# Two vector instructions in place of two GpSimd ones, and small VectorE instructions in other chunks of a fused Mamba, attention and expert kernel

## The reference, cut to what matters

```python
def mamba(x):                                    # x is already layer-normed once
    residual = x
    xz = layernorm(x, in_alpha, in_bias) @ in_proj_w.T + in_proj_b
    x_in, z = split(xz)
    x_conv = silu(causal_conv4(x_in) + conv_b)   # 512 channels
    B, C = split(x_conv @ x_proj_w.T + x_proj_b) # 16 states
    dt = clip(softplus(x_conv @ dt_proj_w.T + dt_proj_b), 1e-4, 10)
    for t in range(1024):
        h = exp(clip(dt * A, -10, 0)) * h + dt * B * x_conv
        if t % 16 == 15: h = h * min(1, 10 / norm(h))      # norm over the 16 states
        y = sum(C * h) + D * x_conv
    out = (y * silu(z)) @ out_proj_w.T + out_proj_b
    return norm_alpha * (residual + out - mean) / (std + 1e-6) + norm_bias   # the closing norm

def experts(x):                                  # 16 experts, the top 6 of a softmax
    p, i = top_k(softmax(x @ router_w.T + router_b), 6)
    gate = scatter(p / (sum(p) + 1e-10), i)
    acc = max(sum(gate), 1e-10)
    return sum(x @ expert_w[e] * gate[e] for e in range(16)) / acc + 1e-10 * sum(p)
```

## Time and profile before

| | |
|---|---|
| median of three runs | 4976.51 us |
| the profiled execution, its time | 4979.03 us |
| its span, first to last instruction | 4977.2 us |
| granted TensorE clock over the span | 0.952 |
| busy: PE, DVE, ACT, POOL | 4396.3, 3774.0, 2928.0, 2691.3 us |
| in 100 to 3150 us (most of the first stage): PE, DVE, ACT, POOL | 2761.8, 2683.7, 2397.4, 2574.0 of 3050 us |
| period of a pair of tiles in the steady loop | about 100 us |

### The profile page before, as it was taken

How to read it: one execution, slowest core, us unless ns; L and a number is a source line. 1 busy time by engine, 2 the same in 40 slices (tenths; PEclk the granted TensorE clock), 3 DMA queues, 4 the chain that set the end, 5 groups by cost and what they waited for, 6 DMA issues and landing times.

```text
span 4977.2 us, 83341 instructions
## 1 busy us (share of the span) xinstructions
PE 4396.3 (88%) x22592; PEld 3061.0 (62%) x22592; DVE 3774.0 (76%) x9556; ACT 2928.0 (59%) x8578; POOL 2691.3 (54%) x1412
## 2 busy tenths in 40 slices
PE   5899998899989998999899989877776779999999
PEld 4777777777777776777677777634434444444444
DVE  3898988888888888888889889953333357777776
ACT  5877787777777777778777778724444421111111
POOL 3888888888888888888888888810000000000000
PEclk8999999999999999999999999988888989999999
DMA  2111111111111111111111111100100100000000
GB/s 95 53 54 49 52 50 52 48 50 51 52 51 47 55 48 55 45 53 49 53 49 53 50 53 49 50 31 26 51 25 30 42 25 19 17 19 18 17 19 16
DMA packets 119406, 214.06 MB, mean 43 GB/s; under 512 B 19232, under 2 KB 85664, under 8 KB 118560
## 3 DMA queue, kind: packets, MB, share of 16 engines
q1 hardware_dynamic: 119072, 211.10, 12.9%
HBM read 184.83 MB, written 26.21 MB: 42 GB/s over the span
## 4 chain that ended last, share of the span: by engine, by line
PE 39%; issue 19%; DVE 17%; POOL 16%; ACT 6%; DMA 1%; DVEq 1%; SPq 1%; POOLq 0%; ACTq 0%
PE ps L644 21%; POOL prod L342 8%; POOL hb L350 5%; DVE macc L957 3%; ACT zr L408 3%; PE ps L771 3%; PE ps L695 2%; PE ps L621 2%; PE ps L674 2%; PE ps L750 2%; DVE sc L1108 1%; DVE dtt L1113 1%; PE ps_dA L771 1%; PE ps L681 1%; POOL u L359 1%
## 5 line engine op out<-in xcount | busy, mean ns | idle before, releaser
L644 PE MATMUL ps<-w_x,mxT 128*128 128x512 f32 x4096 | 1893.1, 601 | 21.8 <-DVE macc L957 21.8
L864 DVE TENSOR_TENSOR_SCAN hb<-ps_dA,hb 128x1088 f32<-128x1088 f32 x512 | 1240.6, 2423 | 164.7 <-issue 103.3
L342 POOL TENSOR_TENSOR prod<-hb,cbc 128x1024 f32<-128x1024 f32 x512 | 1120.2, 2188 | 408.4 <-DVE hb L883 408.4
L408 ACT ACTIVATE zr<-dt,aneg 128x128 f32<-128x128 f32 x4096 | 1240.8, 388 | 69.8 <-DVE dt L1007 69.8
L350 POOL TENSOR_TENSOR hb<-u,bbc 128x1024 f32<-128x1024 f32 x512 | 1199.7, 2343 | 84.2 <-POOL prod L342 72.1
L644 PEld LDWEIGHTS ps<-w_x,mxT 128*128 128x128 f32 x4096 | 745.7, 193 | 725.3 <-issue 654.2
L957 DVE SCALAR_TENSOR_TENSOR macc<-ps,gate,macc 128x256 f32<-128x256 f32 x2048 | 977.5, 477 | 246.9 <-PE ps L644 180.5
L621 PEld LDWEIGHTS ps<-prod,ident 128*128 128x128 f32 x8192 | 979.1, 198 | 254.0 <-POOL prod L342 194.2
L621 PE MATMUL ps<-prod,ident 128*128 128x128 f32 x8192 | 997.1, 282 | 142.5 <-POOL prod L342 142.5
L417 ACT ACTIVATE ps_dA<-zr 128x1024 f32<-128x1024 f32 x512 | 518.3, 1012 | 0.0
L424 ACT ACTIVATE sq<-hb 128x64 f32<-128x64 f32 x512 | 159.6, 312 | 450.8 <-DVE hb L864 447.2
(11 more groups left out here) (184 smaller groups left out, 5014.3 us busy)
## 6 DMA issues: line engine op xcount, KB each, us to landing
bbc<-bcd SPq DMA_DIRECT2D x128, 512.0 KB, 3.8
cbc<-bcd SPq DMA_DIRECT2D x128, 512.0 KB, 3.5
xt<-in_x SPq DMA_DIRECT2D x128, 128.0 KB, 3.0
x2d<-macc SPq DMA_DIRECT2D x64, 128.0 KB, 1.7
xcv<-x2d SPq DMA_DIRECT2D x64, 128.0 KB, 2.1
x3d<-x1b SPq DMA_DIRECT2D x64, 128.0 KB, 1.9
x1b<-x3d SPq DMA_DIRECT2D x64, 128.0 KB, 2.0
out_dram<-macc SPq DMA_DIRECT2D x64, 128.0 KB, 1.7
```

The source lines that it names most:

```text
L342: TT(dst, states, cc, ALU.mult).then_inc(M["prodp"], 1)
L408: last = act(zr[k][:, s, :], dt[:, s // N, :], ACT.Relu, bias=10.0, scale=aneg[:, s:s + 1])
L644: last = mm(banks[p % len(banks)][:], mxT[k][:, j, :], w_x[:, j, p * 512:(p + 1) * 512], start=(j == 0), stop=(j == KD - 1))
L864: V.tensor_tensor_scan(states, dA, states, 0.0, ALU.mult, ALU.add).then_inc(M["scan"], 1)
```

## The change

Five edits. The 20 small tensor_scalar instructions that build the diagonals become two tensor_tensor ones over broadcast operands. o1 moves from chunk 1 to the end of chunk 0. The closing norm is computed as `((oo - mean) * alpha) * (1 / (std + eps)) + beta` by two scalar_tensor_tensor instructions on the DVE, in chunks 3 and 4; the POOL's two are gone, and its residual sum moves from chunk 6 to chunk 7. den is a tensor_scalar with a per-partition scalar instead of a scalar_tensor_tensor; selp moves to just before the gate in chunk 7; route_norm1 moves behind dt's bias, and ACT's side of it behind dt's exp and log. ACT computes the deviation ahead of the squares of chunk 3.

```diff
@@ POOL, extra
-                if c == 4 and "B" in stages:
-                    g.wait_ge(M["o3"], AHEAD + i)
-                    TT(oo[:], oo[:], ga_row[:], ALU.mult).then_inc(M["o4"], 1)
+                if c == 7 and "B" in stages:
                     g.wait_ge(M["o4"], AHEAD + i)
-                    TT(oo[:], oo[:], be_row[:], ALU.add).then_inc(M["o5"], 1)
-                if c == 6 and "B" in stages:
-                    g.wait_ge(M["o5"], AHEAD + i)
                     g.wait_ge(R["ac"], AHEAD + (i - 3) * (X + 1) + 1)
                     TT(x1b[1 - k][:], oo[:], xt[1][:], ALU.add).then_inc(M["x1"], 1)
@@ ACT, step
                 for c in range(NC):
+                    if c == 3 and B:
+                        a.wait_ge(M["vc3"], AHEAD + i)
+                        act(sc[:, 9:10], sc[:, 8:9], ACT.Ln).then_inc(M["ln3"], 1)
+                        a.wait_ge(M["ln3"], AHEAD + i)
+                        act(sc[:, 10:11], sc[:, 9:10], ACT.Exp, scale=0.5).then_inc(M["sd3"], 1)
                     if S_:
                         squares(i, c)
...
-                        if B:
-                            a.wait_ge(M["vc3"], AHEAD + i)
-                            act(sc[:, 9:10], sc[:, 8:9], ACT.Ln).then_inc(M["ln3"], 1)
-                            a.wait_ge(M["ln3"], AHEAD + i)
-                            act(sc[:, 10:11], sc[:, 9:10], ACT.Exp, scale=0.5).then_inc(M["sd3"], 1)
...
                     if c == 7:
-                        if B:
-                            route_norm(i - 1)
                         if F:
                             a.wait_ge(M["dtb"], AHEAD + (i + 3) * EB)
                             act(dtt[:], dtt[:], ACT.Exp).then_inc(M["edt"], 1)
                             a.wait_ge(M["edt"], AHEAD + i + 3)
                             act(dtt[:], dtt[:], ACT.Ln, bias=1.0).then_inc(M["ldt"], 1)
+                        if B:
+                            route_norm(i - 1)
@@ DVE, route_gate (the step with selp is gone from route_step)
+                v.wait_ge(R["router"], AHEAD + n * ROUTER + 6)
+                TT(selp[:], ex[:, 0:X], rest[:, 0:X], ALU.subtract).then_inc(R["router"], 1)
                 v.wait_ge(R["router"], AHEAD + n * ROUTER + 14)
                 TS(gate[k][:], selp[:], ms[:, 11:12], None, ALU.mult).then_inc(R["router"], 1)
@@ DVE, step: chunks 0, 3, 4, 7
                     TS(dt[:], dtt[:], 1e-4, 10.0, ALU.max, ALU.min).then_inc(M["dt"], 1)
+                if B:
+                    v.wait_ge(M["xr"], AHEAD + i * 16)
+                    v.wait_ge(M["x1"], AHEAD + i - 1)
+                    STT(oo[:], xt[1][:], r1b[1 - k][:], ob_row[:], ALU.mult, ALU.add).then_inc(M["o1"], 1)
                 end(0)
...
-                    TS(oo[:], oo[:], mv[:, 2, 0:1], sc[:, 12:13], ALU.subtract, ALU.mult).then_inc(M["o3"], 1)
+                    STT(oo[:], oo[:], mv[:, 2, 0:1], ga_row[:], ALU.subtract, ALU.mult).then_inc(M["o3"], 1)
                 end(3)
...
+                if B:
+                    v.wait_ge(M["o3"], AHEAD + i)
+                    STT(oo[:], oo[:], sc[:, 12:13], be_row[:], ALU.mult, ALU.add).then_inc(M["o4"], 1)
                 end(4)
...
-                    STT(sc[:, 6:7], sc[:, 4:5], 1e-6, sc[:, 5:6], ALU.mult, ALU.add).then_inc(M["den"], 1)
+                    TS(sc[:, 6:7], sc[:, 4:5], 1e-6, sc[:, 5:6], ALU.mult, ALU.add).then_inc(M["den"], 1)
@@ DVE, ahead of the loop
-            for e in range(EB):
-                for t in range(TAPS):
-                    TS(dcw[:, e * TAPS + t, :], ident[:], cw[:, e, t:t + 1], None, ALU.mult).then_inc(s_zero, 1)
-                TS(ddp[:, e, :], ident[:], dpar[:, e:e + 1], None, ALU.mult).then_inc(s_zero, 1)
+            for dst, w in ((dcw, cw[:].rearrange("p e t -> p (e t)")), (ddp, dpar[:])):
+                n = dst.shape[1]
+                TT(dst[:], ident[:].rearrange("p (a c) -> p a c", a=1).broadcast_to([P, n, P]),
+                   w.rearrange("p (a c) -> p a c", c=1).broadcast_to([P, n, P]), ALU.mult).then_inc(s_zero, 1)
```

More of the change, by code:

```diff
@@ L149, in build @@
         dve_m = ("st1", "mv1", "vp", "den", "sx1", "xn", "keep", "xib", "zb", "xcc", "bcv", "dtb", "dt", "scan", "nr",
-                 "st0", "hs", "yg", "o1", "o2", "st3", "mv3", "vc3", "se3", "r3", "o3")
+                 "st0", "hs", "yg", "o1", "o2", "st3", "mv3", "vc3", "se3", "r3", "o3", "o4")
         act_m = ("carry", "lnp", "r1", "qs", "xnTs", "ez", "lz", "ss", "ex", "lx", "sx", "edt", "ldt", "zr", "dA", "sq", "nl",
                  "ne", "ln3", "sd3")
-        pool_m = ("sz", "xcv", "u", "bt", "prodp", "o4", "o5", "x1")
+        pool_m = ("sz", "xcv", "u", "bt", "prodp", "x1")
         pe_m = ("xnT", "xi", "z", "conv", "bc", "dtp", "y", "op")
@@ L447, in route_init @@
             def route_init(n, k, stored):
-                a.wait_ge(R["router"], AHEAD + n * ROUTER + 12)
+                a.wait_ge(R["router"], AHEAD + n * ROUTER + 11)
                 stored()
@@ L923, in route_step @@
                 elif step == 5:
-                    v.wait_ge(R["router"], AHEAD + n * ROUTER + 6)
-                    TT(selp[:], ex[:, 0:X], rest[:, 0:X], ALU.subtract).then_inc(R["router"], 1)
-                elif step == 6:
                     v.wait_ge(R["router"], AHEAD + n * ROUTER + 5)
                     TS(ms[:, 6:7], ms[:, 5:6], ms[:, 4:5], 1e-10, ALU.mult, ALU.add).then_inc(R["router"], 1)
+                elif step == 6:
+                    v.wait_ge(R["router"], AHEAD + n * ROUTER + 7)
+                    V.reciprocal(ms[:, 7:8], ms[:, 6:7]).then_inc(R["router"], 1)
@@ L929, in route_step @@
                 elif step == 7:
                     v.wait_ge(R["router"], AHEAD + n * ROUTER + 8)
-                    V.reciprocal(ms[:, 7:8], ms[:, 6:7]).then_inc(R["router"], 1)
+                    TS(ms[:, 8:9], ms[:, 5:6], ms[:, 4:5], ms[:, 7:8], ALU.mult, ALU.mult).then_inc(R["router"], 1)
                 elif step == 8:
                     v.wait_ge(R["router"], AHEAD + n * ROUTER + 9)
-                    TS(ms[:, 8:9], ms[:, 5:6], ms[:, 4:5], ms[:, 7:8], ALU.mult, ALU.mult).then_inc(R["router"], 1)
+                    TS(ms[:, 9:10], ms[:, 8:9], 1e-10, None, ALU.max).then_inc(R["router"], 1)
@@ L935, in route_step @@
+                    TS(ms[:, 12:13], ms[:, 8:9], 1e-10, None, ALU.mult).then_inc(R["router"], 1)
                 elif step == 9:
                     v.wait_ge(R["router"], AHEAD + n * ROUTER + 10)
-                    TS(ms[:, 9:10], ms[:, 8:9], 1e-10, None, ALU.max).then_inc(R["router"], 1)
-                    TS(ms[:, 12:13], ms[:, 8:9], 1e-10, None, ALU.mult).then_inc(R["router"], 1)
+                    V.reciprocal(ms[:, 10:11], ms[:, 9:10]).then_inc(R["router"], 1)
                 elif step == 10:
-                    v.wait_ge(R["router"], AHEAD + n * ROUTER + 11)
@@ L941, in route_step @@
-                    V.reciprocal(ms[:, 10:11], ms[:, 9:10]).then_inc(R["router"], 1)
-                elif step == 11:
-                    v.wait_ge(R["router"], AHEAD + n * ROUTER + 13)
+                    v.wait_ge(R["router"], AHEAD + n * ROUTER + 12)
                     TS(ms[:, 11:12], ms[:, 4:5], ms[:, 7:8], ms[:, 10:11], ALU.mult, ALU.mult).then_inc(R["router"], 1)
             def route_gate(n, k):
+                v.wait_ge(R["router"], AHEAD + n * ROUTER + 6)
+                TT(selp[:], ex[:, 0:X], rest[:, 0:X], ALU.subtract).then_inc(R["router"], 1)
@@ L1017, in step @@
                 halfway(1)
[L1018 to L1021, removed]
                 end(1)
@@ L1082, in step @@
                     V.bn_stats(st[:, 0, :], xt[0][:]).then_inc(M["st1"], 1)
-                router(5, 6)
                 end(5)
                 start(6)
-                router(6, 7)
+                router(5, 6)
                 if L_:
@@ L1091, in step @@
                     V.bn_aggr(mv[:, 0, :], st[:, 0, :]).then_inc(M["mv1"], 1)
-                router(7, 8)
+                router(6, 7)
                 if L_:
@@ L1097, in step @@
                 halfway(6)
-                router(8, 10)
+                router(7, 9)
                 end(6)
                 start(7)
-                if B:
-                    route_norm1(i - 1, 1 - k, lambda: v.wait_ge(M["x1"], AHEAD + i))
-                router(10, 11)
+                router(9, 10)
                 halfway(7)
@@ L1114, in step @@
                             .then_inc(M["dtb"], 1)
+                if B:
+                    route_norm1(i - 1, 1 - k, lambda: v.wait_ge(M["x1"], AHEAD + i))
                 if L_:
@@ L1117, in step @@
                     V.reciprocal(sc[:, 7:8], sc[:, 6:7]).then_inc(M["sx1"], 1)
-                router(11, 12)
+                router(10, 11)
                 if X_:
@@ L1159, in experts @@
                 route_scores(n0, 0, M0)
-                top(0, 0, range(13))
+                top(0, 0, range(12))
                 tiles(v, tile)
```

8 lines of the change are left out of this document (4 added, 4 removed).

## The result

The changed kernel takes 4841.02 us in the median of four runs (4834.58 to 4842.01) where the kernel before takes 4976.1: the ratio is 0.9724, with a 95% interval from 0.9707 to 0.9741. The forecast was 4938, range 4915 to 4974. The direction was right and the gain more than three times as large, 135 us and not 38.

A forecast was written before the change was run, and what follows sets the result against it. One path of waits through DVE, POOL, ACT and PE bounds each 100 us pair of tiles. 0.76 + 0.76 - 2.73 = -1.21 a pair, -37.5 over 31 pairs, set-up -1.1: -38.6, giving 4938 us, range 4915 to 4974.

The forecast's parts named there:

- third leg of the path: From the end of bound(7) to PE's output projection L674: 9.86 us, or 12.96 where the loop's branch lies between.
- the two legs up to the branch's projection: scan(7) to the end of bound(7), forecast 6.64 us, then on to PE's projection across the branch, forecast 13.34.
- o4 and o1: DVE instructions in chunks 4 and 0, on the path: +0.38 us each per tile, +0.76 each per pair of tiles.
- den: In chunk 7 on the DVE: as a tensor_scalar it takes 0.13 us in place of 0.82, not waiting for the POOL.
- rival 3: den still waits for the POOL until in(0) ends; a pair loses 1.8 us: 5031; chance 0.04.
- selp: Moved to chunk 7 it finds the POOL idle and adds 0.05 us; its removal lets scan(6) start 1.07 earlier.
- o3's wait: Chunk 3: the DVE's 1.1 us wait for ACT goes, o3 waits for the POOL's sz, in PE's shadow: 0.
- the set-up: Ahead of the first tile: two instructions taking 2.9 us replace twenty taking 4.0; -1.1, bounds -2 and 0.
- the POOL's two instructions: Freed, prod(4) follows bound(4) by 0.15 us; the leg to scan(7) becomes 10.83 in both tiles, gaining 0.53 and 1.10.
- H: The end of bound(4), 999.32 us in the even tile, where the path through each tile starts and ends.
- rivals 1: The tile behind the branch loses more PE clock, 0.86 us more, leaving a gain of 0.35 a pair: 4964; chance 0.12.
- rival 2: The odd tile's PE leg also loses clock, 17.41 us growing to 19.1 or 20, 2.0 a pair: 5000; chance 0.09.

The follow-up runs named there:

- o1's experiment: The changed kernel with o1 put back in chunk 1, the loop's position the same: 4785.31 us, ratio 0.9622.
- The experiment: The changed kernel with the closing norm's scale and shift on the POOL again, residual sum in chunk 6, and 4 memsets: 4845.33 us, ratio 0.9742.

## Why the prediction was wrong

**The step that failed** is the third leg of the path, "12.96 (1078.80) where the loop's branch lies between". I carried the branch's wait of 4 us over as a constant, beside a set-up that takes 18 DVE instructions out of the code ahead of it, and gave it neither a bound nor a rival. The wait is the fetch of code: three or four instruction packets start in each. It is there at the positions -4, +12, +14 and +18 and gone at 0, +8 and +128, as it would be if the loop had to lie in three blocks of 128 instructions; the size of a block is inferred. The change happened to move it from +14 to 0; by that rule 12 positions of 128 are good for a loop of 373. With the loop at a position with the wait (+18) the changed kernel takes 4935.72 and 4934.17, where 4938 was forecast; against the kernel before in the same series (4978.63) that is a gain of 43 and 44 us, where 38 was forecast. So 95 of the 135 us are position. By the legs, 77 us of it are the shorter legs at 27 branches, 2.8 at each, and 14 are PE's slow legs, 27 of 56 tiles with the old set-up and 19 in the changed kernel.

In part the 4938 came out by luck. With the old set-up the two legs up to the branch's projection read 7.07 and 12.96, where 6.64 and 13.34 were forecast: only their sum, 20.03 against 19.98, was right.

The Trainium skill has the mechanism ("Runtime: NRT & Kernel Launch", Instruction fetch mechanics): a taken branch to code outside the current window of two blocks waits for a fetch. The runs agree that the loop must fit, not with its blocks of 256 instructions: by two of these a loop of 373 would have 140 good positions in a row (512 - 373 + 1), an estimate from the figure there, and here -4 and +12, only 16 apart, both wait.

**What held, and with which size.**
- o4 and o1 at 0.38 each: 0.40, measured by both legs and by o1's experiment. Neither waits for the POOL; their mean duration is 474 and 473 ns.
- den: it takes 0.20 us and does not wait, as forecast ("under 0.3"), and its type is the reason (rival 3 falls).
- selp: 1.0 a tile, near the sum of its parts in the forecast.
- o3's wait moves from ACT to the POOL's sz (1.16 us in the row above), in PE's shadow, as foreseen. L1060 still waits for PE.
- the set-up: 2.28 and 0.68 us in the trace, 2.9 in all, as forecast.
- the POOL's two instructions: the total was right and the attribution wrong. The prediction gave the legs' 0.53 and 1.10 to the freed POOL, "provided the DVE keeps up, which it does once selp is gone". The experiment shows that with selp gone and the other parts in, H to scan(7) is 10.86 with the norm on the POOL too. Of the gain in this leg selp has 0.50 in both tiles (11.36 with selp back in chunk 5). The odd tile's other 0.57 comes as soon as one of two parts is in, o1 out of chunk 1 or the norm off the POOL: 11.44 with both as before, 10.86 with either. The sum put all of it on the norm, which holds only while o1 stays in chunk 1.
- rivals 1 and 2: with the wait at the branch left in (the old set-up) neither came true. The leg behind the branch stayed at 19.1, and the other at 17.41 in all 28 tiles, though PE had waited 1.95 ahead of it. In the changed kernel PE's wait before the projection is 1.92 to 2.03 in all tiles of the loop, and a third of them lose 1.69, in both parities, which is rival 2's loss together with a gain that it did not foresee. The point from which it decides was put between 1.55 and 2.84; no run had a slow leg behind a wait under 1.9.
- two small slips in the working: scan(6) comes 1.05 earlier and not 1.07, and den at H + 14.67 and not 14.65. Neither moves the sum by more than 1 us.

The clock of such a stretch shows in the granted clock, the column after the engines' busy times; first a tile that is slow, then one that isn't:

```profile
1028.00:1040.00 12.00, 9.07 (x48) 7.23 (x49) 11.44 (x19) 7.59 (x23) 9.96 (x6) 0.88 0.16 57
982.00:994.00 12.00, 10.04 (x60) 7.63 (x60) 11.41 (x21) 8.65 (x26) 9.97 (x5) 1.00 0.17 56
```

PE had waited about as long ahead of both (1.92 and 1.96), so the wait alone doesn't decide. It isn't chance either: in the changed kernel exactly every third tile of the loop is slow, with 8 memsets the slow ones lie two to four tiles apart. What sets the order stays open.

## What to carry to other kernels

Read each wait called "issue" behind a branch as a term of its own, with its price times the number of branches, and look at the count of instruction packets: an edit anywhere ahead of a hardware loop, on the same engine, can add or remove it. Before comparing two versions of a kernel with such a loop, place the loop in the same way in both, or a few padding instructions will outweigh the change. A sum along one path of waits gave 38 us here where 43 and 44 were measured with the branch's wait left in; what it needs is that every leg, also the ones that the change doesn't touch, is asked what could move it.

## What was unexpected of the hardware

- A loop of 373 instructions on the DVE cost 0.2 us at its branch at some positions and 3.9 at others, with 170 and 305 instruction packets in the whole run. The loop of 371 waited 5.0 at -4.
- Four memsets of one element in the right place saved 144 us (5011.85 to 4867.91).
- A second SBUF tensor made an instruction of one element wait for the POOL's running one (1280 ns in the mean against 204).
- TensorE's projection took 3.52 us rather than 1.99 in a third of the tiles, after waits that were all 1.92 to 2.03 us.
